# Mixture of experts: turned rows ahead of the next expert's first product, norms on GpSimd, the choice of experts in two parts

## What the kernel computes

```python
# E = 8 experts, K = 2, DIM = 256, H = 512; xf is layernorm(x), 4096 tokens
gates = softmax(xf @ gate_w)                       # 8 numbers a token
topw, topi = top_k(gates, 2); topw /= sum(topw)
combine = sum(topw[:, :, None] * one_hot(topi, E), axis=1)
h = einsum('td,edh->teh', xf, w1) + b1             # every expert, every token
h = gelu(_ln(h, ln1_g, ln1_b))
y = einsum('teh,ehd->ted', h, w2) + b2
out = einsum('ted,te->td', y, combine)
out = _ln(out + xf, ln_g, ln_b)
# and around it: x + layernorm(out)
```

## Time and profile before

| | |
|---|---|
| median of 3 runs | 5416.48 us (5403.72 to 5419.54) |
| profiled execution | 5420.95 us, its span 5419.2 us |
| mean granted clock of TensorE | 0.934 of full speed |
| busy: PE / DVE / ACT / POOL | 4625.9 / 2720.4 / 1883.4 / 1438.8 us |
| experts' stage | from about 4159 to the end |

### The profile page before, as it was taken

One profiled execution on the slowest core, in us unless ns is written; L12 is line 12 of the kernel. 1 busy time (PEld: TensorE's weight loads), 2 busy tenths in 40 slices (PEclk: granted clock), 3 DMA queues, 4 the chain that ended last, 5 costly groups with the idle time before them and its releaser, 6 DMA issues. The chain is left out here.

```text
span 5419.2 us, 69993 instructions
## 1 busy us (share of the span) xinstructions
PE 4625.9 (85%) x21296; PEld 2818.9 (52%) x21296; DVE 2720.4 (50%) x6103; ACT 1883.4 (35%) x3961; POOL 1438.8 (27%) x1568
## 2 busy tenths in 40 slices
PE   6999999967888699688868858999995999999998
PEld 4666666643444354344434424555553666666665
DVE  4666666644454122454423325565652566566665
ACT  2544444533444311344431114545542121111111
POOL 3333333334555100455520021223212000000100
PEclk9999999988999799899979978999997999999999
DMA  6555555521111111111111122222213000000000
GB/s 92 68 77 78 77 79 76 76 52 33 39 39 35 48 39 38 50 39 39 35 48 35 46 58 69 56 52 60 52 41 88 17 12 12 12 12 12 12 0 12
DMA packets 213587, 245.51 MB, mean 45 GB/s; under 512 B 57012, under 2 KB 173696, under 8 KB 211328
## 3 DMA queue, kind: packets, MB, share of 16 engines
q1 hardware_dynamic: 206080, 239.69, 21.8%
q10 hardware_dynamic: 7296, 3.22, 0.2%
HBM read 89.21 MB, written 33.55 MB: 23 GB/s over the span
## 5 line engine op out<-in xcount | busy, mean ns | idle before, releaser
L766 DVE TENSOR_REDUCE a_neg_max<-a_ps 128x1 f32<-128x384 f32 (+3 forms) x768 | 438.4, 596 | 277.4 <-PE a_ps L508 252.7
L2779 PE MATMUL d_ps_z<-d_w,d_hT 128*128 128x512 f32 x1024 | 511.5, 625 | 33.6 <-DVE d_z L2949 30.6
L2816 PE MATMUL d_ps_y<-d_w,d_gT 128*128 128x256 f32 x2048 | 473.0, 390 | 52.4 <-ACT d_gT L2868 52.4
L2868 ACT ACTIVATE d_gT<-d_ps_t,d_bias,d_gain 128x512 f32<-128x512 f32 x256 | 197.9, 777 | 817.9 <-PE d_ps_t L2793 817.8
L2486 DVE TENSOR_REDUCE c_neg_max<-c_ps 128x1 f32<-128x512 f32 x512 | 340.9, 684 | 254.4 <-PE c_ps L2132 252.9
L2816 PEld LDWEIGHTS d_ps_y<-d_w,d_gT 128*128 128x128 f32 x2048 | 393.8, 195 | 122.6 <-issue 61.1
L2325 ACT ACTIVATE c_probsT<-c_ps 128x512 f32<-128x512 f32 x512 | 299.2, 598 | 396.4 <-PE c_ps L2144 387.6
L1119 PE MATMUL w_ps_e<-w_wqkv,w_hT 128*128 128x512 f32 x768 | 385.4, 627 | 27.1 <-DVE w_crossed L1376 16.4
L654 ACT ACTIVATE a_probs_c<-a_ps 128x512 f32<-128x512 f32 x640 | 355.1, 600 | 124.8 <-PE a_ps L524 101.0
L367 POOL TENSOR_SCALAR_AFFINE_SELECT a_probs_c<-a_probs_c 128x256 f32<-128x256 f32 (+1 forms) x384 | 185.8, 494 | 713.5 <-ACT a_probs_c L654 713.5
L2949 DVE TENSOR_TENSOR d_z<-d_ps_z,d_b 128x512 f32<-128x512 f32 x256 | 176.5, 689 | 369.4 <-PE d_ps_z L2779 369.3
(11 more groups left out here) (281 smaller groups left out, 8737.1 us busy)
## 6 DMA issues: line engine op xcount, KB each, us to landing
a_packed_qk<-a_halves SPq DMA_DIRECT2D x512, 128.0 KB, 4.4
c_packed_qk<-c_halves SPq DMA_DIRECT2D x256, 128.0 KB, 2.3
w_v<-w_v_next SPq DMA_DIRECT2D x16, 1024.0 KB, 4.5
y_dram<-w_out SPq DMA_DIRECT2D x16, 512.0 KB, 3.4
f_y_res<-y_dram SPq DMA_DIRECT2D x16, 512.0 KB, 4.0
d_w<-in_L_ffn_w SPq DMA_DIRECT2D x16, 512.0 KB, 6.3
a_x_in<-in_L_attn_X SPq DMA_DIRECT2D x8, 512.0 KB, 5.3
a_x_res<-in_L_attn_X SPq DMA_DIRECT2D x8, 512.0 KB
```

What stands on the lines that cost most here:

```text
L766: nc.vector.tensor_reduce(neg_max[:, hd // 2 % 2, hd % 2, maps[0]:maps[-1] + 1, i], bank("s", (hd, k))[:, 0:len(maps) * keys].rearrange("p ...
L2779: last = nc.tensor.matmul(ps_z[n % 2][:, :], hT[:, k, t * P:(t + 1) * P], w1[:, e, k, :], start=k == 0, stop=k == KD - 1)
L2816: last = nc.tensor.matmul(ps_y[e % 2][t // 2][:, t % 2, :], gT[:, e % 2, c, t * P:(t + 1) * P], w2[:, e, c, :], start=c == 0, stop=c == KH ...
```

## The change

The stage is rewritten in one form for all engines: `step(b, e, live)` for expert e of batch b, where `live` says which of the batches b-1, b, b+1 exist, `body` runs the eight steps, and `batches` runs `before`, batch 0, a loop over batches 1 to 6, batch 7 and a `drain`. `ref(b, d)` names batch b + d and `following(b, e)` the next expert, if need be expert 0 of the next batch.

- TensorE: in a step `transpose(b, e, c)` stands ahead of the next expert's `hidden(..., c)`. The next batch's input is turned before expert 6's `output`, its gates weighed after it. The weights' turning and the biases' product come in step 1, ahead of and behind its `output`.
- VectorE: `choose` is split into `find_best` (end of step 7 of the batch before) and `choose` (end of step 0); comparisons with the expert's number are four instructions over all tiles instead of eight. acc starts from expert 0's sum and h, the biases are added in step 2. The statistics of the finished batch are taken in steps 0 and 1.
- GpSimd: the norm of the input, both norms of the output, the product with ln_g, the sum with ln_b and the residual's sum run there, in queue with the roots.
- Loads: gain and bias come in as rows (`affine_in`, 64 x 128) and are turned by TensorE; SyncE loads the small ones and expert 0; ScalarE issues the 21 loads of experts 1 to 7 ahead of its other work. Each expert has a semaphore, and TensorE and VectorE wait for one expert at a time, in batch 0.

```diff
+        def expert_weights(e):
+            return [(w1[:, e, :, :], w["w1"][e].rearrange("(k p) h -> p k h", p=P)),
+                    (b1[:, e, :], w["b1"][e].partition_broadcast(P)),
+                    (w2[:, e, :, :], w["w2"][e].rearrange("(k p) h -> p k h", p=P))]
+        def batches(eng, before, body, drain):
+            before()
+            body(0, (0, 1))
+            with eng.Fori(1, B - 1) as b:
+                body(b, (-1, 0, 1))
+            body(B - 1, (-1, 0))
+            drain(B)
...
+            for group, landed in ((gates, gates_in), (expert_weights(0), expert_in[0]), (out, out_in)):
+                for dst, src in group:
+                    sp.dma_start(dst, src).then_inc(landed.sem, 16)
...
+            def norm_input(b, prior):
+                roots_in.step(pool, b, 0, rstd_in[:, :], mv_in[:, :, 1], EPS, neg_half[:, :])
+                standing_wait(pool, roots_in.ready.sem, roots_in.ready.at(b, 1), passed_pool.sem)
+                if prior:
+                    standing_wait(pool, y_read.sem, y_read.at(ref(b, -1), 1), passed_pool.sem)
+                for t in range(NT):
+                    last = nc.gpsimd.tensor_scalar(h[:, t, :], x_in[:, t, :], mv_in[:, t, 0:1], rstd_in[:, t:t + 1],
+                                                   ALU.subtract, ALU.mult)
+                last.then_inc(h_ready.sem, 1)
+            def norm_sums(b):
+                roots_out.step(pool, b, 0, rstd_out[:, :], mv_out[:, :, 1], EPS, neg_half[:, :])
+                standing_wait(pool, roots_out.ready.sem, roots_out.ready.at(b, 1), passed_pool.sem)
+                for t in range(NT):
+                    last = nc.gpsimd.tensor_scalar(y[:, t, :], acc[:, t, :], mv_out[:, t, 0:1], rstd_out[:, t:t + 1],
+                                                   ALU.subtract, ALU.mult)
+                last.then_inc(y_order.sem, 1)
+                pool.wait_ge(y_order.sem, y_order.at(b, 1))
+                nc.gpsimd.tensor_tensor(y[:, :, :], y[:, :, :], ln_g[:, :].unsqueeze(1).to_broadcast([P, NT, D]), ALU.mult)\
+                  .then_inc(y_order.sem, 1)
+                pool.wait_ge(y_order.sem, y_order.at(b, 2))
+                nc.gpsimd.tensor_tensor(y[:, :, :], y[:, :, :], ln_b[:, :].unsqueeze(1).to_broadcast([P, NT, D]), ALU.add)\
+                  .then_inc(y_scaled.sem, 1)
+            def norm_output(b):
+                roots_out.step(pool, b, 1, rstd_out[:, :], mv_out[:, :, 1], EPS, neg_half[:, :])
+                standing_wait(pool, roots_out.ready.sem, roots_out.ready.at(b, 2), passed_pool.sem)
+                for t in range(NT):
+                    last = nc.gpsimd.tensor_scalar(y[:, t, :], y[:, t, :], mv_out[:, t, 0:1], rstd_out[:, t:t + 1],
+                                                   ALU.subtract, ALU.mult)
+                last.then_inc(y_order.sem, 1)
+                standing_wait(pool, res_loaded.sem, res_loaded.at(b, 16), passed_pool.sem)
+                pool.wait_ge(y_order.sem, y_order.at(b, 3))
+                nc.gpsimd.tensor_tensor(x_res[:, :, :], x_res[:, :, :], y[:, :, :], ALU.add).then_inc(y_ready.sem, 1)
+            def step(b, e, live):
+                after, z_next = following(b, e)
+                if 0 in live and (e < E - 1 or 1 in live):
+                    normalise_expert(after, z_next)
+                if e == 0 and -1 in live:
+                    norm_sums(ref(b, -1))
+                if e == 1 and -1 in live:
+                    norm_output(ref(b, -1))
+                if e == 3 and 1 in live:
+                    norm_input(ref(b, 1), 0 in live)
...
+                    if prior:
+                        pe.wait_ge(g_ready.sem, g_ready.at(ref(b, -1), (E - 2) * KH + 3 + k))
...
+            def turn_weights(b):
                 pe.wait_ge(combine_ready.sem, combine_ready.at(b, 1))
-                pe.wait_ge(g_ready.sem, g_ready.at(b, KH))
+                pe.wait_ge(g_ready.sem, g_ready.at(b, 2 * KH))
...
-            def step(z, g, z_after=None, g_after=None):
-                    if z is not None:
-                        hidden(*z, c, z_after)
-                    if c == 0:
-                        pe.wait_ge(zn_ready.sem, zn_ready.at(g[0], g[1] + 1))
-                    transpose(*g, c, g_after)
-                if g[1] == 0:
-                    weigh_biases(g[0])
-                output(*g)
+            def step(b, e, live):
+                after, z_next = following(b, e)
+                more = e < E - 1 or 1 in live
+                if e < E - 1 and -1 not in live:
+                    pe.wait_ge(expert_in[e + 1].sem, 16 * 3)
+                if e == E - 1 and 1 in live:
+                    pe.wait_ge(hT_ready.sem, hT_ready.at(ref(b, 1), 1))
                 for c in range(KH):
+                    if e == E - 1 and c == 1 and 1 in live:
+                        pe.wait_ge(gates_read.sem, gates_read.at(ref(b, 1), 1))
+                    transpose(b, e, c, -1 in live)
+                    if more:
+                        hidden(after, z_next, c, True)
+                if e == 1:
+                    turn_weights(b)
+                if e == E - 2 and 1 in live:
+                    turn_input(ref(b, 1), True)
+                output(b, e, -1 in live)
+                if e == 1:
+                    weigh_biases(b)
+                if e == E - 2 and 1 in live:
+                    weigh_gates(ref(b, 1))
...
+            for e in range(1, E):
+                for dst, src in expert_weights(e):
+                    act.dma_start(dst, src).then_inc(expert_in[e].sem, 16)
...
+            def step(b, e, live):
+                for c in range(KH):
+                    activate(b, e, c, -1 in live)
+                    if e == 0 and c == 1:
+                        weigh_pair(b)
+                if e == 1:
+                    act.wait_ge(combineT_psum.sem, combineT_psum.at(b, 1))
+                    nc.scalar.copy(combineT[:, :], ps_t[1][:, :]).then_inc(combineT_ready.sem, 1)
+                if e == E - 2 and 1 in live:
+                    evacuate_hT(ref(b, 1))
...
+            def find_best(b):
+                standing_wait(dve, gates_read.sem, gates_read.at(b, 1), passed_dve.sem)
                 for t in range(NT):
                     last = nc.vector.max(best[:, t, :], logits[:, t, :])
-                link(last, standing=roots.passed_dve.sem)
+                last.then_inc(best_found.sem, 1)
+                standing_wait(dve, best_found.sem, best_found.at(b, 1), passed_dve.sem)
                 for t in range(NT):
                     last = nc.vector.max_index(index[:, t, :], best[:, t, :], logits[:, t, :])
-                link(last)
-                nc.vector.tensor_copy(index_f[:, :, :], index[:, :, 0:2])
+                last.then_inc(index_found.sem, 1)
...
+            def choose(b):
                 dve.wait_ge(exp_ready.sem, exp_ready.at(b, 1))
-                link(nc.vector.tensor_scalar(pair[:, :, 0:1], pair[:, :, 1:2], 1.0, None, ALU.add))
-                link(nc.vector.reciprocal(pair[:, :, 0:1], pair[:, :, 0:1]))
-                link(nc.vector.tensor_tensor(pair[:, :, 1:2], pair[:, :, 1:2], pair[:, :, 0:1], ALU.mult))
-                for n, dst in ((0, combine), (1, second)):
-                    for t in range(NT):
-                        last = nc.vector.tensor_scalar(dst[:, t, 0:E], iota[:, :], index_f[:, t, n:n + 1],
-                                                       pair[:, t, n:n + 1], ALU.is_equal, ALU.mult)
-                link(last)
+                nc.vector.tensor_scalar(pair[:, :, 0:1], pair[:, :, 1:2], 1.0, None, ALU.add).then_inc(pair_order.sem, 1)
+                for n, dst in ((0, combine[:, :, 0:E]), (1, second[:, :, :])):
+                    last = nc.vector.tensor_tensor(dst, iota[:, :].unsqueeze(1).to_broadcast([P, NT, E]),
+                                                   index_f[:, :, n].unsqueeze(2).to_broadcast([P, NT, E]), ALU.is_equal)
+                last.then_inc(chosen.sem, 1)
...
+            def accumulate(b, e, prior):
+                dve.wait_ge(y_psum.sem, y_psum.at(b, e + 1))
+                if e:
+                    dve.wait_ge(y_read.sem, y_read.at(b, e + 1))
+                else:
+                    dve.wait_ge(combine_ready.sem, combine_ready.at(b, 1))
+                if e == 0 and prior:
+                    dve.wait_ge(y_order.sem, y_order.at(ref(b, -1), 1))
+                for t in range(NT):
+                    last = nc.vector.scalar_tensor_tensor(acc[:, t, :], ps_y[e % 2][t // 2][:, t % 2, :],
+                                                          combine[:, t, e:e + 1], acc[:, t, :] if e else h[:, t, :],
+                                                          ALU.mult, ALU.add)
+                last.then_inc(y_read.sem, 1)
...
+            def step(b, e, live):
+                after, z_next = following(b, e)
+                more = 0 in live and (e < E - 1 or 1 in live)
+                if e == E - 1 and 1 in live:
```

(76 more changed lines are left out.)

326 lines of the change are left out of this document (125 added, 201 removed).

## The result

The changed kernel takes 5261.7 us (median of four runs, 5255.4 to 5271.3), the kernel before 5413.6 beside it (four runs, 5403.7 to 5419.5): a ratio of 0.972, 95% interval 0.970 to 0.974. The profiled execution took 5260.7 us, its span is 5259.0.

What follows compares the result with a forecast made beforehand. TensorE was taken to bound the experts' stage. Start +3, steady sum -147, clock +7 and end +11 gave -126 us, so 5291 us against the runs' median, range 5268 to 5328.

Steps and rivals of the forecast that it cites:

- steady sum: Experts' stage, first second-product to end of the last: 1036 us instead of 1182.95, -147, or -140 with the clock's 7.
- second product: In one expert's step on TensorE: taken at 7.17 us of the step's 15.81.
- clock at the change of batch: TensorE's clock may fall behind the gates: 1 us lost per batch, 7 in all.
- order of the turned rows: In every step with a next one, the last gelu runs beside a 1.72 us product, so 0.93 us goes.
- new wait: Second product waiting for normalised rows in each step: 5.48 us chain under 7.17 of cover, 1.69 left, costed at nothing.
- GpSimd's queue: Norms queued ahead of the experts' roots: step 1's root 1.1 us late, 2.8 us of cover left, no stall.
- Rival (a): GpSimd's queue bounds the change of batch: 5315 at 1.5 times the instruction time, 5380 at twice; chance 0.16.
- the choice in two parts: At the change of batch, removes TensorE's 4.25 us behind the choice, waits on copies and the slow products behind these.
- VectorE and GpSimd in each other's way: The engines disturbing each other in the new order: nothing added; as a bound, 5 us over seven batches.
- Start: From the stage's start to the first second product: 4220 instead of 4217, +3 us; bounds -9 and +8.
- end: From the last root's end to the residual's end: GpSimd's instructions take longer than VectorE's, plus handovers, +11 us.

Runs made afterwards that it cites:

- experiment 1: Kernel before with one edit: TensorE issues the turned rows of group c ahead of the next expert's product c; 5317.0 us, ratio 0.983.
- experiment 2: Kernel after with one edit undone: the next expert's product c stands ahead of the turned rows of group c again; 5338.5 us, ratio 0.986.
- experiment 5: Kernel after with the next batch's input turned behind step 6's second product instead of ahead of it; 5281.1 us, ratio 0.975.
- experiments 6 and 7: Kernel after with four, then eight, more tensor_scalar instructions on GpSimd in the sums' norm; 5299.4 and 5341.3 us, ratios 0.979 and 0.988.
- experiment 3: Kernel after with the choice undivided at the end of VectorE's step 0, ScalarE's exponential behind step 0's last gelu; 5263.4 us.
- experiment 4: Kernel after with the undivided choice and the sums' statistics ahead of expert 1's normalised rows on VectorE; 5320.1 us, ratio 0.982.

## Why the prediction was wrong

The step that failed is the steady sum, by two of its terms: the second product, put at 7.17 us and measured at 6.91, and the clock at the change of batch, put at a loss of 7 us and measured at none. The first alone put the time outside the range: its lower bound, 5268, already had no loss by the clock in it, and 16 us less for the second products would have made it 5252.

*The order of the turned rows*: the mechanism is right, the size not. The sum took the second product at 7.17, from rows that all stood behind the gelu's wait, and removed the wait but not the slower start behind it. In a dense stream it is 6.91 (experiments 1 and 2), 0.26 x 63 steps = 16 us, two thirds of the miss. The number could be read before. Where the edge of a window cuts a second product of the kernel before, its last 22 instructions take 0.216 us each, and 32 of these are 6.91:

```profile
4389.80 4.75 PE d_ps_y L2816 x22
```

*The clock at the change of batch*: taken at 1 us per batch, measured 0: 7 us. The reason given, that the clock may stay when the idle spells go, is borne out by experiment 5: with one spell of 0.72 us put back it falls in four changes of seven.

*The new wait* for normalised rows: none, as forecast; of its margin some 1.3 us are left, now against 6.91. *GpSimd's queue*: its root for expert 2 was forecast 1.1 us late, and the wait of VectorE is 1.25; the forecast 2.8 us of cover left are 2.4. Rival (a)'s prices were too low: beyond the margin the waits of 2.36 and 6.9 us per batch cost 1.5 and 2.6 by the clock as well (experiments 6 and 7).

*What removed the 4.25 us*: the prediction gave it to the choice in two parts. That is wrong as a cause, though the term was right: the halves are worth 0.1 us per batch (experiment 3). What matters is where VectorE does the choice and the sums' statistics: ahead of expert 1's normalised rows they cost 7.0 (experiment 4). The input turned ahead of the second product is worth 1.0 or 2.7 (experiment 5), the order of the turned rows 9.1 (experiment 2). These prices are each of one edit against the kernel after and need not add up; against the kernel before the order is worth 11.5 (experiment 1). The rows of the kernel before give the whole. The batch from 4369.02 to 4520.02 takes 21.6 us more than 129.36: seven gelu waits with the slower start behind them 8.3; at the change of batch five waits (for the turned input 0.73, the logits 0.43, d_z 4.25, a gelu 0.96, the turned weights 0.68) 7.1; and three groups at lower clock, two first products (3.59 and 3.66 us instead of 1.72) and expert 0's second product (8.79 for the one at 4369.02, instead of 6.91), 5.7. Together 21.1. The granted clock is 0.62 from 4520 to 4524, in the next second product of that kind. Of the three slow groups the prediction named the two first products; the slow second product stood in its rows, unnamed, and a third of the loss by the clock was there.

*VectorE and GpSimd in each other's way*: no loss seen, as forecast; in the steady part GpSimd's norm lies beside the taking of products. Where experiment 4 puts VectorE's normalising beside GpSimd's tensor_scalar, four of them take 2.60 us instead of 1.92, and GpSimd's four 5.20 instead of 4.85. The Trainium skill ("SBUF — State Buffer", on the engine ports) has the shared port as an exclusive lock that fully blocks the second for a whole instruction, if VectorE's runs in a two-port mode or has two SBUF inputs; no row names the mode. The rows show a loss, but of 0.68 us over four instructions, and one of VectorE's (4369.89 to 4370.66) lies whole inside one of GpSimd's (4369.69 to 4371.06; spans on GpSimd are rough), so it was not blocked to that one's end.

*Start* (+3, measured +1.8) and *end* (+11, measured +10.9): right; ScalarE's copy came 29.2 us behind the first issue where 31 were forecast. Start 1, steady 17, clock 7: the 25 us between -126 and -151.

## What to carry to other kernels

Take the duration of a group of matmuls from a stretch where it follows work without a wait: a row behind a wait carries the slower start, and an edit that removes the wait removes both. When TensorE is the bound, price a new wait with the clock behind it (0.9 us between dense products cost none here, 2.36 us cost 1.5 more), and ask which instruction on the other engine stands ahead of the one it needs: moving that one is worth more than shortening it. Work that the steady part hides shows up at the start and the end, so let the engine that is free and quicker there do it.

## What was not expected of the hardware

A wait of TensorE of 2.36 us was followed by 1.5 us of loss at lower clock, one of 4.03 us by some 3 us, and 0.72 us ahead of the gates by 1.7 us in four of seven batches and nothing in three. The issue of one load held ScalarE's queue for up to 4.39 us while other loads were in flight, and with it the copies behind; on SyncE the same loads held nothing that was waited for. Small loads came 4.3 us earlier when the large ones were issued behind them.
